# LayerNorm tiles of four batches transposed by VectorE and SyncE's transfers instead of TensorE, in an attention and FFN kernel

## The reference

```
x = x + attention(layernorm(x), ctx, ctx, ...)
x = x + ffn(layernorm(x), ...)

def ffn(h, ...):                                   # h: 16 x 128 x 1024
    query = h @ Wq.T                               # 64 columns
    scores = (query @ Wr.T) @ (keys @ Wr.T).T / sqrt(48) + log_rel      # 256 slots
    w = softmax over the 8 best slots of (query @ keys.T / 8 + log_rel)
    aux = (w @ values) @ Wvd.T @ Wvu.T
    learned = gelu(h @ Wu1.T + bu1) @ Wu2.T        # 256 hidden units
    gate = sigmoid(0.5 * clip(...(learned, log1p(var(h)))...) - 1), 0 if < 0.05
    return h + gate * aux
```

## Time and profile before

| what | value |
| --- | --- |
| median of 3 runs | 640.03 us |
| the profiled execution | 640.05 us |
| its span in the profile | 638.1 us |
| PE busy | 615.7 us (96% of the span) |
| DVE busy | 540.2 us (85%) |
| ACT busy | 416.9 us (65%) |
| POOL busy | 371.7 us (58%) |
| share of PE in the chain that ended last | 92% |
| share of L543, the transposes of h, in that chain from 500 to 600 us | 14% (two rows of 7.0%) |

### The profile page before, as it was taken

How to read it: one execution, slowest core, us unless ns; L and a number is a source line. 1 busy time by engine, 2 the same in 40 slices (tenths; PEclk the granted TensorE clock), 3 DMA queues, 4 the chain that set the end, 5 groups by cost and what they waited for, 6 DMA issues and landing times.

```text
span 638.1 us, 11806 instructions
## 1 busy us (share of the span) xinstructions
PE 615.7 (96%) x3974; PEld 541.3 (85%) x3974; DVE 540.2 (85%) x757; ACT 416.9 (65%) x844; POOL 371.7 (58%) x369
## 2 busy tenths in 40 slices
PE   4899999999999999999999999999999999999796
PEld 3778888888888988888888988888888999999574
DVE  5989898989989898989898989898986745756997
ACT  5566676666666766666676767676664866773793
POOL 4954464848474748474747575756646456421394
PEclk9999999999999999999999999999999999999999
DMA  8943543444444444444444344543245100000056
GB/s 283 252 121 101 144 110 118 118 125 115 126 109 126 111 134 114 126 115 122 112 129 135 108 109 127 150 109 99 72 104 149 42 1 2 1 2 1 34 230 264
DMA packets 52010, 72.57 MB, mean 114 GB/s; under 512 B 10112, under 2 KB 42400, under 8 KB 51696
## 3 DMA queue, kind: packets, MB, share of 16 engines
q1 hardware_dynamic: 50912, 68.07, 37.3%
q0 software_dynamic: 896, 2.45, 1.3%
q10 hardware_dynamic: 144, 1.31, 0.6%
HBM read 29.85 MB, written 8.39 MB: 60 GB/s over the span
## 4 chain that ended last, share of the span: by engine, by line
PE 92%; DVE 3%; SPq 2%; issue 1%; ACT 1%; DMA 1%; DVEq 0%; ACTq 0%
PE ob L504 18%; PE gm L481 17%; PE turn L465 8%; PE k_slot L439 5%; PE q_slot L439 5%; PE k_slot L441 5%; PE q_slot L441 4%; PE gm L556 4%; PE k_slot L440 4%; PE q_slot L440 4%; PE turn L556 4%; PE gm L490 2%; PE turn L512 2%; SPq L383 2%; PE turn L680 1%
## 5 line engine op out<-in xcount | busy, mean ns | idle before, releaser
L967 POOL TENSOR_TENSOR qs_sb<-qs_sb,qrec 128x1024 f32<-128x1024 f32 x64 | 122.0, 1906 | 150.0 <-DVE qrec L1137 150.0
L736 ACT ACTIVATE ek<-k_slot,nkm 128x1024 f32<-128x1024 f32 x62 | 69.1, 1114 | 95.7 <-DVE nkm L1102 95.4
L504 PE MATMUL ob<-mt_sb,q_hd 128*128 128x128 f32 x1024 | 126.4, 277 | 0.6 <-ACT o_sb L758 0.5
L504 PEld LDWEIGHTS ob<-mt_sb,q_hd 128*128 128x128 f32 x1024 | 121.8, 192 | 5.2 <-issue 3.6
L481 PE MATMUL gm<-ekT,ctxT 128*128 128x256 f32 x512 | 118.2, 379 | 1.1 <-DMA ekT<-kt 1.1
L481 PEld LDWEIGHTS gm<-ekT,ctxT 128*128 128x128 f32 x512 | 97.0, 190 | 16.2 <-DMA ekT<-kt 1.5
L746 ACT ACTIVATE qs_sb<-qs_sb 128x1024 f32<-128x1024 f32 x64 | 68.5, 1071 | 31.6 <-DVE qs_sb L1126 31.6
L1102 DVE TENSOR_REDUCE nkm<-k_slot 128x1 f32<-128x1024 f32 x62 | 74.2, 1198 | 16.3 <-PE k_slot L441 16.3
L1133 DVE TENSOR_REDUCE qsum<-qs_sb 128x16 f32<-128x1024 f32 x64 | 76.9, 1202 | 4.1 <-ACT qs_sb L746 4.1
L1126 DVE TENSOR_TENSOR qs_sb<-q_slot,qm 128x1024 f32<-128x1024 f32 x64 | 78.4, 1225 | 2.2
L1109 DVE STREAM_TRANSPOSE kt<-ek 128x1024 f32<-128x1024 f32 x64 | 78.5, 1227 | 0.0
(11 more groups left out here) (200 smaller groups left out, 1227.4 us busy)
## 6 DMA issues: line engine op xcount, KB each, us to landing
ekT<-kt SPq DMA_DIRECT2D x496, 64.0 KB, 2.0
ctx_in<-ctx_rows SPq DMA_DIRECT2D x16, 512.0 KB, 4.6
x_all<-x SPq DMA_DIRECT2D x16, 512.0 KB, 3.6
ctxT<-ctx_cols SPq DMA_DIRECT2D x16, 512.0 KB, 4.1
out<-q_hd SPq DMA_DIRECT2D x15, 512.0 KB, 2.6
Wuq_in<-Wuq_cols ACTq DMA_DIRECT2D x1, 1280.0 KB, 6.5
x_all<-values_cols POOLq DMA_DIRECT2D x1, 1024.0 KB, 8.6
ekT<-kt POOLq DMA_DIRECT2D x16, 64.0 KB, 4.4
```

What stands on the lines that cost most here:

```text
L504: last = nc.tensor.matmul(ob[:, (j % 4) * C:(j % 4 + 1) * C], q_hd[:, t, j * P:(j + 1) * P], mt_sb[:, b % 2, t, :], start=(t == 0), stop=( ...
L967: nc.gpsimd.tensor_tensor(e, e, qrec[:, i % 2, :].unsqueeze(2).broadcast_to([P, PAIR, DH]), ALU.mult).then_inc(q_mul, 1)
```

## The change

Batches 9, 11, 13 and 15 (`TURNED`, t = 0 to 3) are no longer transposed by PE. For each of them:

- ACT writes the normalised rows into a slice of the unused `q_hd` (`h_scale_early(t)`), in steps 3, 5, 7 and 9, instead of into `hbuf` in steps 7, 9, 11 and 13;
- DVE transposes the slice in 32x32 blocks into another slice (`h_turn(t)`), at the end of steps 4, 6, 8 and 10;
- SP issues 16 transfers of 32 partitions x 256 values (32 KB) each, which carry the blocks to their partitions in `Wuq_in`;
- high and low of the batch then read `Wuq_in` in SBUF and not a PSUM slot.

Turning in blocks leaves the 1024 values of h in another order over tiles and partitions than PE's transposes do. So the rows of the weights are permuted on the host, and for the other 12 batches `h_scale` writes `hbuf` in permuted chunks of 32 values; high and low of all batches go through the tile in pieces of 4x8x32. The number of values is the same everywhere. Waits on `h_done` and `h_T` now count only the 12 batches that PE transposes (`by_pe`).

```diff
+TURNED = (9, 11, 13, 15)
...
+        def h_rows(t):
+            return q_hd[:, t % 2, :]
+        def h_blocks(t):
+            return q_hd[:, 2 + t % 2, :]
+        def h_quads(t):
+            raw = Wuq_in[:, :, :].rearrange("p j u -> p (j u)")
+            return raw[:, t % 2 * N:(t % 2 + 1) * N].rearrange("p (a f) -> p a f", a=QUAD)
+        def by_pe(b):
+            return sum(n not in TURNED for n in range(b + 1))
+        def h_source(b, k):
+            if b in TURNED:
+                return h_quads(TURNED.index(b)).rearrange("p a (j r) -> p a j r", r=BLK)
+            return slot[k][:, :].rearrange("p (j a r) -> p a j r", j=J, r=BLK)
+        def h_half(half, k):
+            return hT[half][:, k, :, :].rearrange("p j (a r) -> p a j r", r=BLK)
...
+            sp.wait_ge(wuq_hi, 1)
+            sp.wait_ge(wuq_lo, 1)
+            for t in range(len(TURNED)):
+                sp.wait_ge(h_turned, t + 1)
+                if t >= 2:
+                    sp.wait_ge(hT_hi_done, TURNED[t - 2] + 1)
+                    sp.wait_ge(hT_lo_done, TURNED[t - 2] + 1)
+                for q in range(QUAD):
+                    for a in range(QUAD):
+                        sp.dma_start(h_quads(t)[q * BLK:(q + 1) * BLK, a, :],
+                                     h_blocks(t)[a * BLK:(a + 1) * BLK,
+                                                 q * J * BLK:(q + 1) * J * BLK]).then_inc(h_moved[t % 2], 16)
...
             def h_transpose(b, k):
-                pe.wait_ge(h_done, b + 1)
+                pe.wait_ge(h_done, by_pe(b))
...
-                if b + 1 < B:
+                if b + 1 < B and b + 1 not in TURNED:
...
             def h_scale(b, k):
                 act.wait_ge(nb2_done, b + 1)
-                wait(act, h_T, b - 1)
-                nc.scalar.activation(hbuf[:, k, :], X[:, b, :], ACT.Identity, bias=nb2[:, b, :],
+                if b >= 2:
+                    act.wait_ge(h_T, by_pe(b - 2))
+                nc.scalar.activation(hbuf[:, k, :].rearrange("p (j q r) -> p q j r", j=J, q=QUAD),
+                                     X[:, b, :].rearrange("p (q j r) -> p q j r", q=QUAD, j=J), ACT.Identity, bias=nb2[:, b, :],
                                      scale=rstd2[:, b, :]).then_inc(h_done, 1)
+            def h_scale_early(t):
+                b = TURNED[t]
+                act.wait_ge(nb2_done, b + 1)
+                act.wait_ge(rstd2_done, b + 1)
+                act.wait_ge(o_prod, 4 * B)
+                wait(act, h_turned, t - 1)
+                nc.scalar.activation(h_rows(t), X[:, b, :], ACT.Identity, bias=nb2[:, b, :],
+                                     scale=rstd2[:, b, :]).then_inc(h_early, 1)
             def hT_high(b, k):
-                act.wait_ge(h_T, b + 1)
+                if b in TURNED:
+                    t = TURNED.index(b)
+                    act.wait_ge(h_moved[t % 2], MOVED * (t // 2 + 1))
+                else:
+                    act.wait_ge(h_T, by_pe(b))
                 wait(act, units_prod, b - 1)
-                nc.scalar.copy(hT[0][:, k, :, :], slot[k][:, :].rearrange("p (j c) -> p j c", j=J)).then_inc(hT_hi_done, 1)
+                nc.scalar.copy(h_half(0, k), h_source(b, k)).then_inc(hT_hi_done, 1)
...
-                if b + 2 < B:
+                if b + 2 < B and b + 2 not in TURNED:
                     h_scale(b + 2, b % 2)
+                if b + 6 in TURNED:
+                    h_scale_early(TURNED.index(b + 6))
...
             def hidden_sum(b):
-                pool.wait_ge(h_done, b + 1)
+                if b in TURNED:
+                    pool.wait_ge(h_early, TURNED.index(b) + 1)
+                else:
+                    pool.wait_ge(h_done, by_pe(b))
...
+            def h_turn(t):
+                dve.wait_ge(h_early, t + 1)
+                wait(dve, h_moved[t % 2], MOVED * (t // 2))
+                V.transpose(h_blocks(t), h_rows(t)).then_inc(h_turned, 1)
             def hT_low(b, k):
                 dve.wait_ge(hT_hi_done, b + 1)
                 wait(dve, units_prod, b - 1)
-                V.tensor_tensor(hT[1][:, k, :, :], slot[k][:, :].rearrange("p (j c) -> p j c", j=J),
-                                hT[0][:, k, :, :].bitcast(F32), ALU.subtract).then_inc(hT_lo_done, 1)
+                if b in TURNED:
+                    t = TURNED.index(b)
+                    dve.wait_ge(h_moved[t % 2], MOVED * (t // 2 + 1))
+                V.tensor_tensor(h_half(1, k), h_source(b, k), h_half(0, k).bitcast(F32),
+                                ALU.subtract).then_inc(hT_lo_done, 1)
...
+                if b + 5 in TURNED:
+                    h_turn(TURNED.index(b + 5))
...
-        "Wuq_cols": tiles(np.concatenate([a["L0_ffn_Wu1"].T, a["L0_ffn_Wq"].T], axis=1)),
+        "Wuq_cols": np.concatenate([a["L0_ffn_Wu1"].T, a["L0_ffn_Wq"].T], axis=1).reshape(
+            QUAD, J, BLK, UQ).transpose(0, 2, 1, 3).reshape(P, J, UQ),
```

More of the change, by code:

```diff
@@ L313, in attention_ffn_kernel @@
         h_T = sem("h_T")
+        h_early = sem("h_early")
+        h_turned = sem("h_turned")
+        h_moved = [sem(f"h_moved{k}") for k in range(2)]
         hT_hi_done = sem("hT_hi_done")
```

## The result

| | median of comparison, us | runs | profiled execution, us | its span, us |
|---|---|---|---|---|
| before | 640.49 (639.61 to 641.71) | 11 | 640.05 | 638.1 |
| after | 644.35 (641.84 to 646.25) | 11 | 642.33 | 640.0 |

The ratio is 1.0052 [1.0038, 1.0066]: the changed kernel is slower. Forecast were 639.0 us and a range of 637.2 to 640.9. The profiled execution of the changed kernel is one of its quicker ones, 2.3 us over that of before where the medians lie 3.9 apart; I explain the 2.3 first and come back to the rest. Of the 2.3 us, 1.9 lie in the span and 0.4 around it (642.33 - 640.0 = 2.33, before 1.95), and for the 0.4 I have no explanation.

What follows compares the result with a forecast made beforehand. The prediction took PE, busy 96% of the span, to bound the kernel. Its terms, -3.16 + 0.35 + 0.14 + 1.60 = -1.07 us, took 640.05 us to a forecast of 639.0 us, range 637.2 to 640.9.

Steps and rivals of the forecast that it cites:

- Transfers, priced at 0: SP's 16 transfers per turned batch: 0.43 to 0.48 us each, 9.6 us to landing, all hidden, cost 0.
- block 1: Batch 11's transfers on SP: claimed to run from 548.1 to 557.7 us, wanted at 560.4, so hidden.
- block 2: Batch 13's transfers on SP: turned by 558.8 us at the latest, landing 568.4, wanted at 568.9, so hidden.
- port block: Steps 8 and 9: low(9) on DVE held off the shared SBUF port by POOL's three sums, P(9) later, +1.60 us.
- transfers late: Rival: SP transfers take 0.71 us each, high(13) and then T(14) wait, +3.1 us, 642.1 us; chance 0.10.
- PE, -3.16: Hidden stage on PE: four transpose groups of 0.79 us each go and nothing takes their place, -3.16 us.
- ACT, +0.35: Step 3 on ACT: the added early scaling delays h_scale(6), on which T(6) waits; P(5) starts 0.35 us later.
- DVE, +0.14: Step 6 on DVE: h_turn(11) delays low(8), so P(8) starts later than PE is free, +0.14 us.
- Pieces, 0: 4x8x32 pieces in high, low and h_scale: claimed to cost 0, at most 0.5 us.

Runs made afterwards that it cites:

- experiment 4: Changed kernel with each of the 64 transfers carrying 16 KB instead of 32, the other half of each block not moved; 646.4 us in a single run.
- experiment 1: Changed kernel with the 64 transfers left out, so the four batches read old contents of `Wuq_in`; 637.58 us, ratio to before 0.9946.
- experiment 2: Changed kernel with all transfers made, but high and low read the blocks before the move, so nothing in the hidden stage waits; 638.17 us, ratio to before 0.9948.
- experiment 7: Changed kernel with four 128 KB transfers a batch instead of 16, `h_scale` writing `hbuf` in values 16 bytes apart; 644.42 us, ratio to before 1.0054.
- experiment 6: Changed kernel with no batch turned, keeping only the pieces of 32 values and the permuted weights; 640.79 us, ratio to before 1.0001.
- experiment 9: The changed kernel run again without an edit, for a second profile; 644.44 us in a single run.
- experiment 3: Changed kernel with 28 unused transposes of `ident` on PE before the one-column product, to keep PE busy in the wait; 643.86 us, ratio to before 1.0042.
- experiment 5: Changed kernel with only three batches, 9, 12 and 15, turned by DVE instead of four; 640.03 us, ratio to before 0.9981.
- experiment 8: Changed kernel with four 128 KB transfers a batch, `hbuf` and weights as before, early scalings reading in steps, batch 9's one step later; 638.79 us, ratio to before 0.9962.
- experiment 10: experiment 8 with all of batches 9 to 15 turned, each scaled five steps ahead; 650.37 us, ratio to before 1.0126.

## Why the prediction was wrong

- **Transfers, priced at 0: the step that failed.** "A plain one took 0.43. The new ones have one run of 256 a partition, so I take 0.43 to 0.48 each." Measured: 0.643. The right row stood in the same group: the burst of 16 that does the same thing in the attention part, 10.23 / 16 = 0.64. I talked it down by shape and bytes, and experiment 4 shows that bytes don't count. Two figures of the text have to be put right first. By its own times block 1 is covered up to (560.4 - 548.1 - 2.0) / 16 = 0.64 us a transfer, not 0.57, and block 2 up to (568.9 - 558.8 - 2.0) / 16 = 0.51, little more than the price taken; and 570.9 in the rival is 559.5 + 11.4, not 558.8 + 11.4. With 0.64 in the working, block 2 lands at 558.8 + 10.2 + 2.0 = 571.0, 2.1 after it is wanted, and with 0.9 of slack the time is 639.0 + 1.2 = 640.2: the row that fitted best gave the sign, barely, and not the size. The rest was hidden by the port block, which put the time at which high(13) is wanted 1.6 us too late. Without it, by the same rows, block 2 is issued from 558.3 (when block 1 has been), lands at 570.6 and is wanted at 567.3: an estimated wait of 3.3 on ACT and 2.4 on PE, measured 3.10 and 2.34. The rival "transfers late" had the chain in full (SP without a break, high(13), the table load, the gelu, h_scale(14), T(14)); it was given 0.10. Experiments 1 and 2 show that it is this wait and nothing else of the transfers.
- **Also missing: what a wait of 3 us does to PE's clock.** Even the rival priced only the wait. The gap was followed by a clock of 0.50, 2.70 us more; together 5.0 of the 5.2 us between experiment 1 and the changed kernel. In experiment 7 it fell behind a wait of 1.92 us as well.
- **The port block, +1.60: wrong.** P(9) started 554.80 - 550.42 = 4.38 us after P(8); the working without the block had 555.25 - 550.86 = 4.39. Two things failed. low(9) ran ahead of POOL's second sum and not behind it, and the one block on `varh` was in the kernel before as well. That two SBUF operands on DVE and a sum on POOL exclude each other, the rule cited from the Trainium skill ("SBUF — State Buffer", "Who interferes with whom"), holds: the second sum took 2.50 us beside low(9). The same section says that issue order decides who blocks, which the prediction left out when it let the port change hands at every operation; low(9), the loser of the forecast, started first, by 0.04 us. `unit_weights` was held longer beside POOL's L1130, 1.73 us at 557.59 where before it took 0.88, but P(10) followed P(9) after 3.75 us, no more than the 3.81 that I had counted: 0.
- **PE, -3.16, ACT, +0.35, DVE, +0.14: right.** T(10) to P(9) is one transpose group, 0.79, as before. T(6) waited for ACT: counted from T(5) it came 0.37 us later than before (4.87 against 4.50) where the working had 0.47, and P(5) 0.31 later (5.72 against 5.41) where it had 0.35. P(8) began 3.72 us after P(7), where T(9) had begun 3.59 after it: 0.13 for the 0.14. From T(6) to P(8) the forecast had 550.86 - 536.57 = 14.29 us, measured 14.33. Their sum alone, 637.4, met experiment 1's 637.25. At the start of P(12) the changed kernel was 2.49 us ahead (566.89 against 569.38 before), and lost it all behind it.
- **Pieces, 0: right** (experiment 6).
- **The two errors had opposite signs**, +1.60 too much and 5.0 too little, so that the forecast missed the profiled time by 3.3 us only: 639.0 - 1.6 + 5.0 = 642.4, measured 642.33. That the two agree to 0.1 is luck in part: T(6) began 0.48 us earlier than forecast, mostly because T(5) did, and the time around the span was 0.38 longer. The median, 644.35, is 5.3 us over the forecast, since an ordinary execution waits longer than the profiled one (experiment 9).

What stays open: why single transfers are slow in some executions, which lengthens the wait (seen in the one profile of experiment 9 that lies near the median), why the clock falls in the output stage and in the attention part in some executions and not in others, and why experiment 3's median fell so little.

## What to carry to other kernels

Price a transfer by the row of the most similar one in the same trace, issued back to back, and count them on their queue up to each deadline; fewer bytes in each don't shorten the queue, fewer transfers do. Where a term changes the sign of the result within its bounds, here at about 0.63 us a transfer with a row at 0.64, that term carries the forecast and needs a chance to match. A doubtful delay elsewhere (here the port block) also moves the deadlines, and can hide a wait that is there without it: work out each uncertain term with the others at 0 too. And a new wait of PE of 2 to 3 us is to be costed with what PE runs slowly behind it, here 2.7 us on top of 2.3.

## What the runs showed of the hardware

- An SBUF-to-SBUF transfer takes SP 0.59 to 0.61 us in the median, whether it carries 16 (591 ns), 32 (591) or 128 KB (605), and in a burst they start 0.63 to 0.65 us apart (four in 2.56 us with 32 and with 128 KB); single ones took 0.9 to 1.5 in seven of the nine profiles with such transfers, so that the mean over 64 was 0.643 to 0.664. The loads took 0.43. Landing takes 1.8 us for 16 and 32 KB, 2.6 for 128.
- The clock fell to 0.50 with PE gaps of 3.25 and 4.63 us in the changed kernel, 5.05 in experiment 4 and 1.92 in experiment 7, there 1.4 us after PE had gone on; with a gap of 1.71 in experiment 3 it did not. After P(15), where PE has little to do for some 4 us in every version, it fell in most profiled executions (experiments 2 to 6 and 8 to 10) and not in others (before, after, experiments 1 and 7).
- ACT takes 2.25 us for 128x1024 values that are read or written 16 bytes apart, 1.23 in pieces of 32 values or in one.
- DVE's low(9), with two operands in SBUF, ran at its usual 1.21 us while a sum of POOL that had started 0.04 us after it took 2.50 instead of 1.23. It came the same way in experiments 1, 2 and 9: the three sums together took 4.91 us in the changed kernel and 4.93, 4.90 and 4.92 there.
